# Four projection stages, a sampled convolution and a norm-and-gate stage rewritten: how their steps overlap, and how TensorE's array is divided

## The chip, the core and the metric

One NeuronCore of a Trainium2 chip runs the whole kernel as one launch. Its engines are TensorE (PE in the profile, with weight loads as PEld), VectorE (DVE), ScalarE (ACT), GpSimd (POOL) and SyncE (SP), which here only issues DMA. The metric is device time in microseconds (us), median of three runs. All data are float32. A float32 matmul stands in the profile as two PE records, so that "x2" of a 384-column matmul is one matmul of the program.

## The reference

Four residual layers run one after the other on x of shape 2 x 96 x 96 x 96 (two images, 96 channels, 9216 places). Each normalises by groups of three channels, goes through a selective scan in four directions and adds its output to x. What the change touches is this (cut to what matters):

```python
x = x + _L0_conv_ref(_gn(x), ...)      # layer 0: xz = in_proj(x); xs, z = split; 3x3 convolution,
                                       # batch norm, gelu, 1x1 to 2 offsets, grid_sample_bilinear, scans
x = x + _L1_conv_ref(_gn(x), ...)      # layer 1: layer norm, softmax gate, four mamba scans
x = x + _L2_conv_ref(_gn(x), ...)      # layers 2 and 3: in_proj, depthwise 3x3, four scans
x = x + _L3_conv_ref(_gn(x), ...)

def _gn(v, G=32, eps=1e-5):            # group statistics over 3 channels x 9216 places
    g = v.reshape(B_, G, C_ // G, H_, W_)
    return ((g - m) / jnp.sqrt(s + eps)).reshape(v.shape)

# layer 1, on the normalised tokens: layer norm over the 96 channels with gain and bias, then
# gate = softmax(w2 @ tanh(w1 @ x + b1) + b2) over 4 directions, w1: 24 x 96, w2: 4 x 24
```

## The kernel before

The stages of a layer run strictly one after another, each a `Phase` that ends with a barrier of all engines: statistics and projection, convolution, preparation of the scan's inputs, scan, merge, finish. Layer 1 has `norm_gate` ahead of its projection and no convolution stage of its own. SP issues all DMA, in program order, on one queue. The scans take most of the time and are the same in both kernels.

**Steps.** All stages here walk the 9216 places in 24 steps of N = 384 places (four image rows). The hidden width is 192 channels for each of two images; they lie in three tiles of 128 partitions: tile 0 is image 0's first 128 channels, tile 1 image 1's, and tile 2 holds the last 64 channels of image 0 in partitions 0 to 63 and of image 1 in 64 to 127. So a product that goes into or comes out of tile 2 uses half of the rows or half of the columns of PE's array, with zeros in the weights for the other half.

**`group_norm_head`** (L282, called by `norm_gate` and by three of the four projections) loads x (2 images, each in 2 halves) and takes `bn_stats` of 36 pieces of 512 places on DVE. All wait for all loads, on one semaphore.

**`project`** (L356, once a layer): each step scales x of both images on ACT (L419; in layer 1 it only copies, L417), then runs eight matmuls on PE (L437 to L440), four into `p_xs` and four into `p_z`, of which two each are tile 2's from image 0 and image 1. DVE copies `p_xs` to SBUF (L451), ACT takes silu of `p_z` (L425), both as one instruction over three banks, and SP stores both. ACT takes step s's silu before it scales step s + 1, and `p_xs` and `p_z` exist once.

**`conv_sampled`** (L556, layer 0): each step runs 63 matmuls of 384 columns (nine taps by seven blocks of `FEEDS`) into `p_conv` (L639), three gelus on ACT (L674), three matmuls into `p_off` (L647), tanh (L680), an affine step on POOL (L624), six matmuls that spread the offsets over partitions (`p_frac`, L657), and eight DVE instructions for each of three tiles (L709 to L727) that interpolate. PE goes through these in this order, and begins the next step's convolution after the spreads. The whole grid and the taps are loaded ahead of the first matmul.

**`norm_gate`** (L127, layer 1): for each step and each image, one after the other, with one buffer of each kind: scale (ACT), mean matmul (PE), subtract (DVE), square (ACT), variance matmul (PE), square root (ACT), reciprocal and product (DVE), gain and bias (ACT), hidden matmul (PE), tanh (ACT), three logit matmuls (PE), softmax (DVE, exp on ACT, DVE), three transposes (PE), copy (DVE). Each waits for the one ahead of it.

Of the kernel before, what the change touches and what calls it, by code (L numbers as in the profile page):

```python
# [10 lines left out]
ALU = mybir.AluOpType  # L11
ACT = mybir.ActivationFunctionType

P = 128
IMAGES = 2
# [12 lines left out]
GATE_HID = CH // 4  # L28
TAPS = 9
# [97 lines left out]
def norm_gate(nc, x_d, w, out_d, gate_d):  # L127

    with Phase(nc, "ng") as ph:
        x, scale, bias, loaded, stats = group_norm_head(nc, ph, x_d, w)  # L130
        N = SUB
        STEPS = L // N
        mean96 = ph.sb("mean96", [CH, CH])
        w1 = ph.sb("w1", [CH, GATE_HID])
        w2 = ph.sb("w2", [GATE_HID, DIRS])
        vecs = ph.sb("vecs", [CH, 2])
        b1 = ph.sb("b1", [GATE_HID, 1])
        b2 = ph.sb("b2", [P, DIRS])
        eye = ph.sb("eye", [P, P])
        xn = ph.sb("xn", [CH, N])  # L140
        xc = ph.sb("xc", [CH, N])
        sq = ph.sb("sq", [CH, N])
        sd = ph.sb("sd", [CH, N])
        rs = ph.sb("rs", [CH, N])
        xl = ph.sb("xl", [CH, 2, N])
        th = ph.sb("th", [GATE_HID, N])
        lg = ph.sb("lg", [P, 3, DIRS])
        mx = ph.sb("mx", [P, 3])
        sm = ph.sb("sm", [P, 3])
        gt = ph.sb("gt", [DIRS, 2, N])  # L150
        p_mean = ph.ps("p_mean", [CH, 512])
        p_var = ph.ps("p_var", [CH, 512])
        p_hid = ph.ps("p_hid", [GATE_HID, 512])
        p_log = ph.ps("p_log", [P, 3, DIRS])
        p_gt = ph.ps("p_gt", [DIRS, 512])
        weights = ph.sem("weights")
        eps_ready = ph.sem("eps_ready")
        act = ph.sem("act")
        dve = ph.sem("dve")
        pe = ph.sem("pe")  # L160
        xl_stored = [ph.sem(f"xl_stored{b}") for b in range(IMAGES)]
        gt_stored = [ph.sem(f"gt_stored{b}") for b in range(IMAGES)]
        A, D, E = 6, 13, 5
        eps = ph.sb("eps", [CH, 1])

        block_cm = ph.block()
        block = block_cm.__enter__()

        @block.sync
        def _(sp):  # L170
            for dst, src in ((mean96, w["mean96"]), (w1, w["gate_w1"]), (w2, w["gate_w2"]), (vecs, w["norm_gb"]),
                             (b1, w["gate_b1"]), (b2, w["gate_b2"]), (eye, w["eye"])):
                sp.dma_start(dst[:], src).then_inc(weights, 16)
            with sp.Fori(0, STEPS) as i:
                for b in range(IMAGES):

                    sp.wait_ge(act, i * (2 * A) + (b * A + 4) + ONE)
# [2195 lines left out]
```

## Time and profile before

| | us |
|---|---|
| median of 3 runs | 30857.21 (30854.06 to 30863.32) |
| the profiled execution | 30855.04 |
| its span | 30853.3 |
| PE busy in the span | 23829.2 |
| DVE busy in the span | 25538.5 |

The profiled execution's time is 1.7 us above its span and 2.2 us below the median. Since the stages are separated by barriers, the page's shares of the whole span say little about the stages changed here; each has to be read in its own stretch: layer 0's projection from 64 to 341 us, the sampled convolution from 392 to 1796, `norm_gate` from 8401 to 9304, layer 1's projection from 9308 to 9608. In a stretch, the columns give each engine's busy time, the granted PE clock as a share of full speed, and the busy share of the DMA engines.

### The profile page before, as it was taken

Reading aid. Unit: us, or ns where it says so; the run is one execution under the profiler, and the core shown is the slowest. Engines: PE = TensorE matmul, PEld = TensorE weight load, DVE = VectorE, ACT = ScalarE, POOL = GpSimd, SP = SyncE. Lnnn points to the kernel's source line nnn. Section 1 sums busy time; section 2 is a strip of 40 time slices with the busy share of each in tenths; the row PEclk is TensorE's granted clock in tenths of the full one; section 3 lists DMA queues with packets and bytes.
Section 4 is the critical chain, followed back from the end, with each engine's and each line's share of the span. In section 5 each row is a group of like instructions: output and inputs, shape, how many; then the busy total and the mean of one; then the engine's idle time right before and its main releaser. Section 6 shows DMA issues by size and latency. Waiting matters only on the chain. (4 is left out here: it accounts for less than half of the span.)

```text
span 30853.3 us, 332186 instructions
## 1 busy us (share of the span) xinstructions
PE 23829.2 (77%) x97030; PEld 7351.8 (24%) x97030; DVE 25538.5 (83%) x16489; ACT 14890.1 (48%) x20203; POOL 22839.6 (74%) x10221
## 2 busy tenths in 40 slices
PE   6877888888435688888886778888883778888885
PEld 3442222222112222222222422222221422222222
DVE  1259999999535999999993799999994689999995
ACT  1045555555134655555531555555551455555552
POOL 0028999999003699999992299999990189999991
PEclk8888888888756688888876888888886888888887
DMA  2042222221504422222235522222215532222224
GB/s 75 10 164 70 45 45 45 49 50 38 178 9 157 160 52 45 45 45 47 52 110 180 208 61 45 45 50 49 45 38 199 189 86 45 51 48 45 45 45 170
DMA packets 1155007, 2419.20 MB, mean 78 GB/s; under 512 B 118600, under 2 KB 656166, under 8 KB 1143680
## 3 DMA queue, kind: packets, MB, share of 16 engines
q1 hardware_dynamic: 1153224, 2397.86, 28.2%
q8 instruction: 821, 13.45, 0.2%
q14 instruction: 962, 7.88, 0.1%
HBM read 1374.43 MB, written 1023.05 MB: 78 GB/s over the span
## 5 line engine op out<-in xcount | busy, mean ns | idle before, releaser
L1355 POOL TENSOR_TENSOR scan_hc<-scan_bc,scan_h 128x1024 f32<-128x1024 f32 x6912 | 16086.7, 2362 | 108.3 <-DVE scan_h L1519 107.3
L1519 DVE TENSOR_TENSOR_SCAN scan_h<-scan_da,scan_state,scan_dbu 128x1024 f32<-128x1024 f32 x6912 | 15987.4, 2338 | 140.1 <-ACT scan_da L1407 133.9
L1438 PE MATMUL scan_da<-scan_dd,scan_ssel 32*128 32x512 f32 x27648 | 9101.0, 745 | 3013.1 <-DVE scan_h L1519 2781.0
L1407 ACT ACTIVATE scan_da<-scan_da,scan_a_cur 128x1024 f32<-128x1024 f32 x6912 | 7516.7, 1087 | 7720.6 <-PE scan_da L1438 7714.2
L1438 PE MATMUL scan_p_du<-scan_dd,scan_ssel 32*128 32x512 f32 x27648 | 9198.0, 745 | 534.2 <-DMA scan_bc<-bc_d 214.2
L1506 DVE TENSOR_TENSOR scan_dbu<-scan_p_du,scan_bc 128x1024 f32<-128x1024 f32 x4608 | 5561.0, 1207 | 506.1 <-PE scan_p_du L1438 475.5
L1341 POOL TENSOR_TENSOR scan_dbu<-scan_bc,scan_dus 128x1024 f32<-128x1024 f32 x2304 | 5446.0, 2364 | 145.7 <-ACT scan_dus L1381 145.1
L1438 PEld LDWEIGHTS scan_da<-scan_dd,scan_ssel 32*128 32x128 f32 x27648 | 2450.3, 216 | 10296.4 <-DVE scan_h L1519 8730.6
L1455 PE MATMUL scan_p_y<-scan_hc,scan_rsel 128*32 128x512 f32 x27648 | 4778.1, 772 | 17.2 <-POOL scan_hc L1355 16.8
L1438 PEld LDWEIGHTS scan_p_du<-scan_dd,scan_ssel 32*128 32x128 f32 x27648 | 2409.9, 211 | 3617.2 <-DVE scan_dbu L1506 2962.3
L1386 ACT ACTIVATE scan_state<-scan_h,scan_a_cur 128x1 f32<-128x1 f32 x6912 | 2025.1, 293 | 1584.3 <-DVE scan_h L1519 1476.4
L1381 ACT ACTIVATE scan_dus<-scan_p_du 128x1024 f32<-128x1024 f32 x2304 | 2358.5, 1024 | 217.2 <-PE scan_p_du L1438 170.1
L404 POOL MEMSET proj_xs_o<- 128x2352 f32 x4 | 8.2, 2058 | 2493.8 <-POOLq L69 2493.8
L835 POOL COPY prep_useq<-prep_grid 128x576 f32<-128x576 f32 (+1 forms) x480 | 581.3, 1263 | 1487.9 <-DMA du_d<-prep_useq 914.2
L1455 PEld LDWEIGHTS scan_p_y<-scan_hc,scan_rsel 128*32 128x32 f32 x27648 | 597.5, 119 | 3228.0 <-issue 2359.3
L639 PE MATMUL conv_p_conv<-conv_grid,conv_taps 128*128 x3024 | 1030.7, 504 | 52.6 <-DMA conv_grid<-xs_d 52.6
L624 POOL TENSOR_SCALAR conv_frac<-conv_frac 4x384 f32<-4x384 f32 x24 | 12.1, 504 | 1414.8 <-ACT conv_frac L680 1414.8
L451 DVE COPY proj_xs_o<-proj_p_xs 128x1152 f32<-128x1152 f32 x96 | 130.4, 1358 | 1006.8 <-PE proj_p_xs L440 1006.8
L845 PE MATMUL prep_p_dbl<-prep_useq,prep_wx 128*128 128x384 f32 x1728 | 805.1, 631 | 168.6 <-POOL prep_useq L835 168.6
L714 DVE TENSOR_TENSOR conv_top<-conv_diff,conv_p_frac 128x384 f32<-128x384 f32 x72 | 39.9, 554 | 1064.4 <-PE conv_p_frac L657 1062.7
L639 PEld LDWEIGHTS conv_p_conv<-conv_grid,conv_taps 128*128 128x128 f32 x3024 | 593.7, 197 | 500.2 <-issue 121.3
L1162 DVE SCALAR_TENSOR_TENSOR prep_useq<-prep_raw,prep_tapv,prep_useq 128x768 f32<-128x768 f32 x432 | 650.2, 1515 | 55.5 <-ACT prep_useq L1119 45.4
(215 smaller groups left out, 14787.6 us busy)
## 6 DMA issues: line engine op xcount, KB each, us to landing
scan_bc<-bc_d SPq DMA_DIRECT2D x576, 512.0 KB, 12.1
du_d<-prep_useq SPq DMA_DIRECT2D x384, 576.0 KB, 3.8
delta_d<-prep_delta SPq DMA_DIRECT2D x384, 576.0 KB, 4.3
scan_dd<-delta_d SPq DMA_DIRECT2D x1152, 192.0 KB, 4.9
scan_dd<-du_d SPq DMA_DIRECT2D x1152, 192.0 KB, 6.7
y_d<-scan_y SPq DMA_DIRECT2D x576, 384.0 KB, 5.8
merge_y<-y_d SPq DMA_DIRECT2D x384, 576.0 KB, 5.8
xs_d<-proj_xs_o SPq DMA_DIRECT2D x96, 588.0 KB, 3.3
```

Of the source, the lines that this page charges most:

```text
L639: last = nc.tensor.matmul(p_conv[:, m, 0:N], taps[:, tap, blk, :], grid[:, src, bass.ds(i * (2 * ROWS) + (j * ROWS + dy), ROWS), dx:dx + S ...
L845: last = nc.tensor.matmul(p_dbl[v % 2][:, 0:N], wx[:, v // (CHUNKS * PIECES), m, :], piece(v)[:, m, :], start=(m == 0), stop=(m == 2))
L1162: nc.vector.scalar_tensor_tensor(out=own, in0=raw[:, m, tap:tap + DW], scalar=tapv[:, m, tap:tap + 1], in1=own, op0=ALU.mult, op1=ALU.add) ...
L1341: nc.gpsimd.tensor_tensor(dbu[:, u % DBU_SLOTS, :], bc[:, s, image(u % UNITS), :], dus[:, u // TRIO % DUS_SLOTS, :], ALU.mult).then_inc(sh ...
L1355: nc.gpsimd.tensor_tensor(hc[:, u % HC_SLOTS, :], c, h[:, u % H_SLOTS, :], ALU.mult).then_inc(hc_ready, 1)
L1381: nc.scalar.activation(dus[:, u // TRIO % DUS_SLOTS, :], p_du[:], ACT.Copy).then_inc(share_copied, 1)
L1386: nc.scalar.activation(state[:, v % UNITS:v % UNITS + 1], h[:, v % H_SLOTS, T - 1:T], ACT.Copy, scale=a_cur[:, s, UNITS:UNITS + 1]).then_i ...
L1407: nc.scalar.activation(da[u % DELTA_BANKS][:], da[u % DELTA_BANKS][:], ACT.Exp, scale=a_cur[:, slot(u)[0], u % UNITS:u % UNITS + 1]).then_ ...
L1438: return nc.tensor.matmul(dst[:, half * H:(half + 1) * H], ssel[rows, i, :], dd[rows, s, m, j, :], start=True, stop=True)
L1455: last = nc.tensor.matmul(p_y[n % 2][at:at + QUAD, :], rsel[:, i, :], hc[:, v % HC_SLOTS, half * H:(half + 1) * H], start=(v % EIGHT < PAI ...
L1506: nc.vector.tensor_tensor(dbu[:, u % DBU_SLOTS, :], p_du[:], bc[:, slot(u)[0], image(u % UNITS), :], ALU.mult).then_inc(dbu_ready, 1)
L1519: nc.vector.tensor_tensor_scan(h[:, v % H_SLOTS, :], da[v % DELTA_BANKS][:], dbu[:, v % DBU_SLOTS, :], state[:, v % UNITS:v % UNITS + 1], ...
```

## The change

**Projection.** The eight PSUM banks are used in turn, one for each tile of a step (`bank_of`), each with its own semaphore count, so that PE runs on as soon as the bank of eight tiles ago is empty. Tile 2's two matmuls now write 64 columns each, in the two halves of the array's columns. ACT scales step s + 1 before step s's silus. In layer 1, x is not copied but read directly, and comes in four quarters, each with its semaphore. The stores have four buffers. All steps are written out.

**Sampled convolution.** `convolve_low` does tiles 0 and 1: for each tap two full matmuls and two of 64 rows each (tile 2 as the source), in the two halves of the array's rows. `convolve_high` does tile 2: for each tap two matmuls of 64 columns each and one full one. The offsets of step s - 1 come between low and high of step s, the spreads after high or between the two; the two spreads of a tile stand in rows 0 to 3 and 32 to 35. The grid is loaded in four bands, the first ahead of the taps.

**Norm and gate.** Scale and centring go into one matrix (`scaled_c`), the gain into the matrix that spreads the reciprocal (`gamma`), both images go together through most instructions, the reciprocal is taken of 2 rows in place of 96, and seven steps are in flight: turn t does the first part for step t and the last for step t - 6. There is a preamble that computes `scaled_c` and `shift`.

**Group statistics.** Each half of x has its own semaphore, so `bn_stats` begins with the first half.

In the part on `norm_gate` the three loops are those of TensorE, ScalarE and VectorE, in this order.

```diff
 def project(nc, l, x_d, w, xs_d, z_d, normed):
+        def bank_of(s, half, m):
+            return bank[(s * 2 * TILES + half * TILES + m) % BANKS]
...
-                            nc.tensor.matmul(psum[:, 0, 0:N], win[:, half, 0, :], xn[:, j, 0, :], start=True, stop=True)
-                            nc.tensor.matmul(psum[:, 1, 0:N], win[:, half, 0, :], xn[:, j, 1, :], start=True, stop=True)
-                            nc.tensor.matmul(psum[:, 2, 0:N], win[:, half, 1, :], xn[:, j, 0, :], start=True, stop=False)
-                            nc.tensor.matmul(psum[:, 2, 0:N], win[:, half, 2, :], xn[:, j, 1, :], start=False,
-                                             stop=True).then_inc(done, 1)
+                        for b in range(IMAGES):
+                            free(s, half, b)
+                            nc.tensor.matmul(bank_of(s, half, b)[:, 0:N], win[:, half, 0, :], src[b], start=True, stop=True).then_inc(done, 1)
+                        free(s, half, 2)
+                        for b in range(IMAGES):
+                            rows = slice(b * HALF, (b + 1) * HALF)
+                            last = nc.tensor.matmul(bank_of(s, half, 2)[rows, 0:N], win[:, half, 1 + b, rows], src[b], start=True, stop=True)
+                        last.then_inc(done, 1)
...
 def conv_sampled(nc, w, xs_d, u_d):
-        FEEDS = [[(0, 0), (2, 1)], [(1, 0), (2, 2)], [(0, 3), (1, 4), (2, 5)]]
...
+                def convolve_low(s):
+                    t.wait_ge(rows_loaded[band(s)], 16 + ONE)
+                    t.wait_ge(gelu_done, max(s * TILES - 1, 0) + ONE)
+                    for tap in range(TAPS):
+                        first, end = tap == 0, tap == TAPS - 1
+                        for m in range(2):
+                            nc.tensor.matmul(p_conv[:, m, 0:N], taps[:, tap, 0, :], rows_of(s, m, tap), start=first, stop=False)
+                        for m in range(2):
+                            half = slice(m * HALF, (m + 1) * HALF)
+                            last = nc.tensor.matmul(p_conv[:, m, 0:N], taps[half, tap, 1 + m, :], rows_of(s, 2, tap)[half],
+                                                    start=False, stop=end)
+                            if end:
+                                last.then_inc(conv_done, 1)
+                def convolve_high(s):
+                    t.wait_ge(gelu_done, s * TILES + ONE)
+                    for tap in range(TAPS):
+                        for m in range(2):
+                            half = slice(m * HALF, (m + 1) * HALF)
+                            nc.tensor.matmul(p_conv[half, 2, 0:N], taps[:, tap, 3 + m, half], rows_of(s, m, tap),
+                                             start=(tap == 0), stop=False)
+                        last = nc.tensor.matmul(p_conv[:, 2, 0:N], taps[:, tap, 5, :], rows_of(s, 2, tap), start=False,
+                                                stop=(tap == TAPS - 1))
+                    last.then_inc(conv_done, 1)
...
+                for s in range(STEPS + 2):
+                    if s < STEPS:
+                        convolve_low(s)
+                    if 0 <= s - 1 < STEPS:
+                        offsets(s - 1)
+                    if 0 <= s - 2:
+                        spread_offsets(s - 2, 2)
+                    if s < STEPS:
+                        convolve_high(s)
+                    if 0 <= s - 1 < STEPS:
+                        for m in range(2):
+                            spread_offsets(s - 1, m)
...
 def norm_gate(nc, x_d, w, out_d, gate_d):
+                for t in range(TURNS):
+                    if step(t):
+                        centre_x(t)
+                    if step(t - 1):
+                        square_sum(t - 1)
+                    if step(t - 2):
+                        spread(t - 2)
+                    if step(t - 3):
+                        hide(t - 3)
+                    if step(t - 4):
+                        make_logits(t - 4)
+                    if step(t - 6):
+                        transpose(t - 6)
...
+                for t in range(TURNS):
+                    if step(t - 1):
+                        deviation(t - 1)
+                    if step(t):
+                        square(t)
+                    if step(t - 2):
+                        add_beta(t - 2)
+                    if step(t - 3):
+                        hyperbolic(t - 3)
+                    if step(t - 4):
+                        exponential(t - 4)
...
+                for t in range(TURNS):
+                    if step(t - 5):
+                        soft_divide(t - 5)
+                    if step(t - 2):
+                        scale_x(t - 2)
+                    if step(t - 4):
+                        soft_shift(t - 4)
+                    if step(t - 1):
+                        invert(t - 1)
+                    if step(t - 6):
+                        take_gates(t - 6)
...
 def group_norm_head(nc, ph, x_d, w):
-                        d.wait_ge(loaded, 16 * 5 + ONE)
+                        d.wait_ge(half_loaded[2 * b + n // (NBN // 2)], 16 + ONE)
                         nc.vector.bn_stats(bn[:, b, n, :], x[:, b, n * BN:(n + 1) * BN]).then_inc(stats, 1)
```

On PE, the sampled convolution of a step stands as follows before (the numbers are output partitions x columns; `p_off` is 4 partitions high):

```order
L639 MATMUL conv_p_conv<-conv_grid,conv_taps 128x384 x29
L645 REGISTER_ALU
L647 MATMUL conv_p_off<-conv_gel,conv_off_w 4x384 x3
L650 ISA
L655 ISA
L657 MATMUL conv_p_frac<-conv_frac,conv_off_sel 128x384 x4
L655 REGISTER_ALU
L657 MATMUL conv_p_frac<-conv_frac,conv_off_sel 128x384 x2
```

Of the change, the same engine from the last taps of `convolve_low` of a step to the first of `convolve_high`, and the place where one step's high ends and the next step's low begins:

```order
L787 MATMUL conv_p_conv<-conv_grid,conv_taps 128x384 x2
L790 MATMUL conv_p_conv<-conv_grid,conv_taps 128x384 x2
L812 MATMUL conv_p_off<-conv_gel,conv_off_w 36x384 x3
L822 MATMUL conv_p_frac<-conv_frac,conv_off_sel 128x384 x2
L801 MATMUL conv_p_conv<-conv_grid,conv_taps 64x384 x2
L803 MATMUL conv_p_conv<-conv_grid,conv_taps 128x384
...
L803 MATMUL conv_p_conv<-conv_grid,conv_taps 128x384
L822 MATMUL conv_p_frac<-conv_frac,conv_off_sel 128x384 x4
L787 MATMUL conv_p_conv<-conv_grid,conv_taps 128x384 x2
```

The offsets and spreads have moved from the end of a step, where nothing else stood on PE, to places between the halves of the next one; and whole-array matmuls (L787, L803) now alternate with pairs in halves (L790, L801).

On ACT, one image of a step of `norm_gate` before, and one whole turn (both images) of the change:

```order
L196 ACTIVATE ng_xn<-ng_x,ng_gbias,ng_scale 96x384
L199 REGISTER_ALU
L200 ACTIVATE ng_sq<-ng_xc 96x384
L202 ISA
L203 ACT_TABLE_LOAD
L203 ACTIVATE ng_sd<-ng_p_var,ng_eps 96x384
L205 REGISTER_ALU
L206 ISA
L207 ACTIVATE ng_xl<-ng_xc,ng_vecs 96x384
L209 REGISTER_ALU
L210 ACT_TABLE_LOAD
L210 ACTIVATE ng_th<-ng_p_hid,ng_b 24x384
```

```order
L297 ACT_TABLE_LOAD
L297 ACTIVATE ng_sd<-ng_p_v,ng_eps 2x384
L305 ACTIVATE ng_xc<-ng_p_c,ng_shift 96x384
L306 ACTIVATE ng_sq<-ng_p_c,ng_shift 96x384
L305 ACTIVATE ng_xc<-ng_p_c,ng_shift 96x384
L306 ACTIVATE ng_sq<-ng_p_c,ng_shift 96x384
L313 ACTIVATE ng_xl<-ng_xr,ng_vecs 96x768
L319 ACT_TABLE_LOAD
L319 ACTIVATE ng_th<-ng_p_hid,ng_b 64x384
L323 ACTIVATE ng_lg<-ng_lg 128x24
```

The two table loads, which stood in each image's chain, now stand once a turn for both images, and the instructions of a turn belong to five different steps.

## Rows read from the trace of the kernel before

**Rows 1.** By stretch: us; PE, PEld, DVE, ACT, POOL busy (count); PE clock, DMA share, GB/s.

```profile
64.00:341.00 277.00, 186.19 (x384) 97.70 (x384) 32.58 (x24) 85.23 (x94) 0.00 (x0) 0.80 0.28 101
348.00:392.00 44.00, 0.00 (x0) 0.00 (x0) 0.00 (x0) 1.13 (x1) 0.60 (x2) 0.50 0.97 410
392.00:1796.00 1404.00, 1249.08 (x3456) 673.07 (x3456) 309.18 (x581) 70.33 (x109) 12.09 (x24) 0.90 0.03 10
8466.00:9304.00 838.00, 331.34 (x720) 120.40 (x720) 269.32 (x624) 311.90 (x408) 0.00 (x0) 0.50 0.03 9
9308.00:9345.00 37.00, 0.00 (x0) 0.00 (x0) 0.00 (x0) 0.59 (x1) 2.06 (x1) 0.50 0.92 199
9345.00:9608.00 263.00, 180.17 (x384) 94.37 (x384) 32.59 (x24) 77.53 (x96) 0.00 (x0) 0.80 0.28 105
16995.00:17186.00 191.00, 187.05 (x569) 105.57 (x567) 186.72 (x354) 37.43 (x69) 0.00 (x0) 1.00 0.29 112
```

**Rows 2.** Timeline of one projection step: start, duration, instruction, [idle before, releaser].

```profile
328.90 1.13 ACT L425 ACTIVATE proj_z_o<-proj_p_z 128x1152 f32<-128x1152 f32 x1
329.93 1.29 ACT L419 ACTIVATE proj_xn<-proj_x,proj_gbias,proj_scale 96x384 f32 x2
331.35 1.64 PE L437 MATMUL proj_p_xs<-proj_xn,proj_win 96*128 96x384 f32 x2 [3.85 <-ACT proj_xn L419]
340.15 1.13 ACT L425 ACTIVATE proj_z_o<-proj_p_z 128x1152 f32<-128x1152 f32 x1 [8.93 <-PE proj_p_z L440]
```

**Rows 3.** Timeline of the sampled convolution, PE, its first and last step.

```profile
392.67 42.62 PE L639 MATMUL conv_p_conv<-conv_grid,conv_taps 128*128 x126 [52.56 <-DMA conv_grid<-xs_d]
...
1727.85 42.34 PE L639 MATMUL conv_p_conv<-conv_grid,conv_taps 128*128 x126
1772.08 2.10 PE L647 MATMUL conv_p_off<-conv_gel,conv_off_w 128*4 128x384 f32 x6 [1.89 <-ACT conv_gel L674]
1775.59 2.84 PE L657 MATMUL conv_p_frac<-conv_frac,conv_off_sel 4*128 4x384 f32 x8 [1.42 <-POOL conv_frac L624]
```

**Rows 4.** Timeline, PE, layer 0's finish: rows*columns of the array.

```profile
8058.94 0.81 PE L1990 MATMUL fin_p_c<-fin_ym,fin_centre 128*128 128x384 f32 x2
8059.59 0.81 PE L1991 MATMUL fin_p_c<-fin_ym,fin_centre 128*128 128x384 f32 x2
...
8062.17 0.81 PE L1995 MATMUL fin_p_c<-fin_ym,fin_centre 128*128 128x384 f32 x2
8062.90 2.20 PE L2002 MATMUL fin_p_r<-fin_rs,fin_gamma 2*128 2x384 f32 x6
8065.03 0.89 PE L2010 MATMUL fin_p_o<-fin_t,fin_wo 128*96 128x384 f32 x2
```

**Rows 5.** Timeline, PE: groups in quarters of the array's rows and columns.

```profile
1908.47 2.84 PE L855 MATMUL prep_p_dt<-prep_dtv,prep_wdt 13*128 13x384 f32 x12 [1.73 <-ACT prep_dtv L876]
...
5007.87 1.07 PE L1455 MATMUL scan_p_y<-scan_hc,scan_rsel 128*32 128x512 f32 x8
```

**Rows 6.** Timeline, ACT: the nearest to the changed kernel's instructions.

```profile
436.68 1.80 ACT L674 ACTIVATE conv_gel<-conv_p_conv,conv_shift,conv_scale 128x384 f32<-128x384 f32 x3
...
1907.86 1.03 ACT L876 ACTIVATE prep_dtv<-prep_p_dbl,prep_ones 128x384 f32<-128x384 f32 x2
...
9700.66 1.01 ACT L1119 ACTIVATE prep_useq<-prep_raw,prep_conv_b,prep_tapv 128x768 f32<-128x768 f32 x1
```

**Rows 7.** Norm and gate: two steps' starts (timeline), then groups by line.

```profile
8466.99 0.71 ACT L196 ACTIVATE ng_xn<-ng_x,ng_gbias,ng_scale 96x384 f32 x1
...
8501.92 0.71 ACT L196 ACTIVATE ng_xn<-ng_x,ng_gbias,ng_scale 96x384 f32 x1
...
L203 ACT ACT_TABLE_LOAD x48 | 61.6, 1283 | 0.9
...
L255 DVE RECIPROCAL ng_rs<-ng_sd 96x384 f32<-96x384 f32 x48 | 122.3, 2549 | 136.9 <-ACT ng_sd L203 136.9
```

**Rows 8.** Timeline, DVE, head of the first projection.

```profile
35.11 21.45 DVE L315 BATCH_NORM_STATS2 proj_bn<-proj_x 96x6 f32<-96x512 f32 x36 [33.77 <-DMA proj_x<-in_x]
```

More of the change, by code:

```diff
@@ L294, in group_norm_head @@
     eps5 = ph.sb("eps5", [CH, 1])
-    loaded = ph.sem("x_loaded")
+    loaded = ph.sem("avg_loaded")
+    half_loaded = [ph.sem(f"x_loaded{n}") for n in range(2 * IMAGES)]
     stats = ph.sem("x_stats")
@@ new lines, in _ @@
+                if not normed:
+                    normalise(0)
+                for s in range(STEPS):
+                    if not normed and s + 1 < STEPS:
+                        normalise(s + 1)
+                    a.wait_ge(z_stored[s % DEEP], 16 * (s // DEEP) + ONE)
+                    for m in range(TILES):
+                        a.wait_ge(z_psum, s * TILES + m + 1 + ONE)
+                        nc.scalar.activation(z_o[:, s % DEEP, m, :], bank_of(s, 1, m)[:, 0:N], ACT.Silu).then_inc(z_ready, 1)
@@ new lines, in offsets, with spread_offsets @@
+                def offsets(s):
+                    t.wait_ge(gelu_done, (s + 1) * TILES + ONE)
+                    t.wait_ge(tanh_done, s + ONE)
+                    for m in range(TILES):
+                        last = nc.tensor.matmul(p_off[:, 0:N], off_w[:, m, :], gel[:, m, :], start=(m == 0), stop=(m == 2))
+                    last.then_inc(off_done, 1)
+                def spread_offsets(s, m):
+                    v = s * TILES + m
+                    t.wait_ge(frac_ready, s + 1 + ONE)
+                    t.wait_ge(lerp, max(v - 1, 0) * STEP + ONE)
+                    for axis in range(2):
+                        q = OFF_ROWS[axis]
+                        last = nc.tensor.matmul(p_frac[v % 2][:, axis, 0:N], off_sel[q:q + 2 * IMAGES, axis, m, :],
+                                                frac[q:q + 2 * IMAGES, s % 2, :], start=True, stop=True)
+                    last.then_inc(spread, 1)
@@ L661, in _, with gelu @@
             @block.scalar
             def _(a):
-                a.wait_ge(loaded, 16 * 7 + ONE)
+                def gelu(s, m):
+                    a.wait_ge(conv_done, s * TILES + m + 1 + ONE)
+                    a.wait_ge(off_done, s + ONE)
+                    nc.scalar.activation(gel[:, m, :], p_conv[:, m, 0:N], ACT.Gelu, bias=shift[:, m:m + 1],
+                                         scale=scale[:, m:m + 1]).then_inc(gelu_done, 1)
+                a.wait_ge(loaded, 16 * 4 + ONE)
                 a.wait_ge(consts, 1 + ONE)
```

612 lines of the change are left out of this document (342 added, 270 removed).

## The prediction

> **What bounds the kernel now.** I read first the busy times by stretch, then the timeline of a single step in each stretch, because barriers separate the stages: what a stage loses is lost outright, and what it gains is gained outright. The scans, preparations, merges and finishes are not touched, so I leave them at their times.
>
> In none of the changed stages does an engine work through. Layer 0's projection has PE busy 186 of 277 us at a mean granted clock of 0.80, ACT 85 and DVE 33, and the DMA engines 28% [rows 1]. The timeline says why: the silu of a step begins only 8.93 us after ACT's last work, when PE has finished; then ACT scales the next step, and PE waits 3.85 us for that [rows 2]. PE and ACT take turns, 24 times: 277 / 24 = 11.5 us a step.
>
> The sampled convolution has PE busy 1249 of 1404 us [rows 1]. Its 24 convolutions run from 392.67 to 1770.2 (1727.85 + 42.34), so 1377.5 us, with 23 tails between them [rows 3]. A step's 63 matmuls take 42.3 us; the period is (1770.2 - 435.3) / 23 = 58.0 us. The other 15.7 us are gelu, offsets, tanh, POOL's step, spreads and the interpolation that frees their banks, all in line.
>
> `norm_gate` is a pure chain: in 838 us PE is busy 331, ACT 312, DVE 269, and the clock is 0.50, the lower of its two levels (1.2 GHz), throughout [rows 1]. A step of both images takes 8501.92 - 8466.99 = 34.9 us [rows 7].
>
> **PE's prices, which carry the sum.** One matmul of 384 columns at full clock (2.4 GHz) takes 8059.59 - 8058.94 = 0.645 us when the next has the same shape. When the shape changes from 128*128 to 2*128, the step is 8062.90 - 8062.17 = 0.73, so 0.09 more; and the three matmuls of the new shape then take 2.13 us to the next group in place of 1.935, which is 0.20 more: 0.09 for leaving and 0.11 because the first weights of a new shape are loaded in the open [rows 4]. I take 0.20 us a change, and 0.15 where the new shape has 64 columns or fewer, since fewer weight columns are loaded; bounds are 0.09 and 0.20 for these. Whether a half of the array (64 rows or columns) counts as a new shape, no row shows; the bounds are 0 and 0.20, and I take 0.20, since the rows that change to a quarter are the nearest.
>
> Do halves run together? Twelve records of 13 rows each, six matmuls, take 2.84 us, where one after another they would take 3.87; the order in the code (rows 64, 96, 64, and again) allows four slots, 2.58. And eight records of 32 columns, four matmuls of 512 columns, take 1.07 us, where the same in turn would take four times 0.86 [rows 5]. I take full overlap: a pair costs one slot of 0.645.
>
> Here the Trainium skill has a rule that speaks against the change: TensorEngine Tiling (Array Packing), section Tiling Modes, says that changing the tiling mode, not just the tile, drains TensorE. The trace agrees, with the 0.20 us above. By the page's table of speedups alone (up to 2 times for 64 rows or columns, nothing for changes) the time would be that of the first rival.
>
> **Sampled convolution.** Per tap, low has 2 full matmuls and a pair, high a pair and a full one: 5 slots in place of 7, so 45 a step; offsets 3, spreads 3 (a pair each): 51 slots, 32.9 us. Changes of shape: 18 in low, 18 in high, 1 for the offsets, 2 for spreads: 39, of them 10 at 0.15, so 7.3 us. That is 40.2 us a turn, in place of 58.0. Does anything stop PE? Low of step s needs gelu of tiles 0 and 1 of s - 1, done during high; high needs tile 2's gelu of s - 1, done during low; the spreads come some 15 us after the offsets, and the chain between them was 3.5 us (1775.59 - 1772.08) [rows 3]. DVE's 309 us in all [rows 1] are 12.9 a step. So PE runs through, and stays at full clock: a stretch of 191 us that runs through had 1.00 [rows 1]. 24 x 40.2 = 965, less 3 for the first turn, which has no offsets, plus 2 for its first matmuls at half clock: 964 against 1377.5, **413 saved**. The tail after the last convolution stays. The start: all 17.9 MB were awaited, 44 us at 410 GB/s [rows 1]; now one band of four and the taps, 7.2 MB, 18 us and a landing: **24 saved**.
>
> **Projections of layers 0, 2 and 3.** Six slots, 3.87 us, and four changes (two at 0.15), 0.70: 4.57 a step. Beside it ACT has two scalings (1.29, [rows 2]) and three silus (three gelus of the same size take 1.80, [rows 6]), 3.1 us, and DVE three copies (33 us / 24 = 1.36 as one, some 1.6 as three). The stores: 28% of 277 / 24 is 3.2 us of DMA time a step. All are under 4.57, so PE is the bound. A bank is wanted again after eight tiles, 6 us later. 24 x 4.57 = 110, 3.5 for the first 7 us at half clock, 1 for the last silu: 114 against 277. 3 x 163 = **489 saved**. POOL's zeroing is twice as long (four pieces), some 2 us more, and lies beside the first scalings.
>
> **Layer 1's projection.** PE did nothing in the stage's first 37 us, while both images landed at 199 GB/s, and then the steps took 263 [rows 1]. A quarter of x lands after 9 us and the weights ahead of it after 2: PE starts 26 us earlier. The steps take 114, as above: 149 saved. The first stores queue behind the last quarters of x, until some 36 us in; step 4 wants the first store's buffer at about that time, so I charge 4. 149 + 26 - 4 = **171 saved**.
>
> **Norm and gate.** ACT's turn: two table loads 2.57, square root and tanh 0.57 each at most (0.60 by the gelus), four of centre and square at 0.515 (1.03 for two), gain and bias over 768 columns 1.01, exp 0.2: 7.0 us [rows 6, 7]. PE's turn at full clock: seven slots (the pair for both images counts once) 4.5, six small matmuls 1.1, six changes 0.8: 6.4 us. DVE: the reciprocal of 2 rows is as long as that of 96, 2.55 [rows 7], now once for both images, and some 2.8 more: 5.4. The binding loop is ACT alone; the loop through PE (last square, centring, sum of squares, root, squares again) is 0.2 + 1.3 + 0.2 + 1.3 + 0.6 + 2.1 = 5.7. So 7.0 a turn; PE at 6.4 of 7.0 stays nearly always busy, and I take full clock after the first turns. 24 x 7.0 = 168, 14 for six draining turns (a chain of one step), 6 for the start at half clock: 188; preamble and three more loads 3. 838 - 191 = **647 saved**.
>
> A page says otherwise on the table loads: ScalarE: Activation LUTs, What ACT_TABLE_LOAD costs, gives 1283 ns and a drain of 1380 for each switch. The trace has the 1283 but only 0.9 us of idle ahead of all 48 [rows 7], so it doesn't agree on the drain; by the page the stage would be 66 us longer.
>
> **Heads.** x lands over 33.8 us, then 36 pieces take 21.45 [rows 8]. Now three quarters of that lie beside the load, and 5.4 are left: 16 us, four times, **64 saved**.
>
> Sum: 413 + 24 + 489 + 171 + 647 + 64 = 1808. From the profiled execution's 30855.0 that is 29047; the median was 2.2 higher, so 29049. I predict 29050.
>
> **The rivals.**
> *Halves are no new shape* (12%). For it: all rows that show a change go to a quarter or less of the rows or columns. Against: nothing in particular but that the drain is there at all. Then the 17 changes inside low and the 17 inside high cost nothing, 6.4 us a turn, 154, and 0.70 x 96 = 67 in the projections: 28830.
> *Halves don't overlap* (8%). Against it are both rows of 5; for it, that they show quarters. It costs 18 slots a convolution turn, 279, and 2 a projection step, 124: 29450.
> *PE stays at 1.2 GHz in `norm_gate`* (12%). For it: the clock was 0.50 for 838 us [rows 1], and small matmuls and changes are gaps of a kind. Then PE's turn is 12.8 us and binds: 24 x 5.8 = 139 more, 29190.
> *Slower than before* (2%): a change of shape between half and whole arrays costs far more than one to a quarter. There are 39 x 24 + 4 x 96 = 1320 of them; to eat 1808 us each must cost 1.4 us more than the 0.2 taken. From 1.6 us on it decides. At 1.8 us the kernel would take 31150. Rows 4 show nothing near it.
>
> My forecast has 66%, with its own range 28930 to 29180 (ACT's or PE's turns 5% off). **Range** at 8 in 10: 28790 to 29310; it takes in the clock rival, and the first at its edge, and leaves out the second and the last. What a measurement of this kernel can tell from no change is about 0.2%, 62 us: faster 0.97, same 0.01, slower 0.02.
>
> **What would show it.** In the profile after: convolution turns of 40 us with PE running through at clock 1.00, and steps of 0.73 to 0.85 us where L790 follows L787; projection steps of 4.6 us; `norm_gate` turns of 7 us with ACT busy throughout. I'd be wrong if L787 follows L790 at 0.645, if a pair takes 1.29, or if in a projection PE waits for banks (L575 behind L550).

## The result, and the profile after

The changed kernel takes 29517.14 us (median of 4 runs, 29504.46 to 29548.98) against 30855.64 of the kernel before (4 runs, 30836.15 to 30863.32): ratio 0.9568, 95% interval 0.9553 to 0.9584. That is 1338 us less where 1808 were forecast. The time lies 207 us above the forecast range.

The profiled execution took 29522.75 us (span 29520.9), 1332 less than that of before. The stages are separated by barriers, so each difference can be read by itself, from a stage's first to its last instruction:

| stage | before, us | after, us | saved | forecast |
|---|---|---|---|---|
| four heads | 59.1, 59.4, 59.2, 59.0 | 42.6, 42.1, 42.5, 43.0 | 66 | 64 |
| sampled convolution | 1446.5 | 1011.4 | 435 | 437 |
| projections 0, 2, 3 | 283.8, 282.9, 284.2 | 215.2 each | 205 | 489 |
| projection 1 | 304.7 | 223.7 | 81 | 171 |
| `norm_gate` behind its head | 844.8 | 254.7 | 590 | 647 |
| all the others | | | -45 | 0 |

Two lines are right to 2 us. The projections miss 374 us between them, `norm_gate` 57, and the stages that nobody touched are 45 us longer; together that is the gap.

The windows of the changed kernel answer to [rows 1]. The columns are the same: PE, PEld, DVE, ACT and POOL busy with counts, granted clock, DMA share, GB/s.

```profile
291.10:1245.00 953.90, 953.90 (x3420) 352.29 (x3420) 289.74 (x528) 54.79 (x95) 11.68 (x23) 1.00 0.06 23
7955.00:8202.00 247.00, 236.63 (x602) 84.65 (x602) 116.91 (x220) 152.44 (x235) 0.00 (x0) 0.60 0.10 30
8218.00:8427.00 209.00, 208.14 (x384) 70.71 (x384) 40.16 (x72) 36.03 (x72) 0.00 (x0) 0.50 0.47 159
15486.00:15694.00 208.00, 207.85 (x384) 70.71 (x384) 40.16 (x72) 62.20 (x116) 1.50 (x2) 0.50 0.36 135
```

PE now works through in the convolution and the projections, as intended: 953.90 of 953.90 us in the one, 208.14 of 209.00 and 207.85 of 208.00 in the others; in `norm_gate` it is busy 236.63 of 247.00. But the clock column differs. The convolution has 1.00; the projections have 0.50 from end to end, the lower level (1.2 GHz). Before, with PE idle for a third of the same stage and every matmul of the one shape 96*128, the projections had a mean of 0.80 [rows 1]. `norm_gate` has 0.60.

The timeline of PE in layer 2's projection is the answer to [rows 2]. A step is now two groups of full columns and two pairs of halves. (A *slot* below is the time of one matmul of 384 columns, a *change* a change of shape, that is of the rows*columns in use.)

```profile
15549.72 1.55 PE L579 MATMUL proj_bank<-proj_xn,proj_win 96*64 96x384 f32 x4
15551.20 2.93 PE L575 MATMUL proj_bank<-proj_xn,proj_win 96*128 96x384 f32 x4
15554.06 1.55 PE L579 MATMUL proj_bank<-proj_xn,proj_win 96*64 96x384 f32 x4
15555.53 2.93 PE L575 MATMUL proj_bank<-proj_xn,proj_win 96*128 96x384 f32 x4
15558.39 1.55 PE L579 MATMUL proj_bank<-proj_xn,proj_win 96*64 96x384 f32 x4
```

No row shows an idle time, so PE waits for no bank and no operand. Start to start, a step takes 15558.39 - 15549.72 = 8.67 us, where 4.57 were forecast. (A record is half a matmul here: x4 are two matmuls of full columns, or one pair.) The pair begins at 15549.72 and the full ones at 15551.20, 1.48 later: it takes one slot, not two, at a slot of 1.28 us at this clock, and 0.20 for the change. Halves do lie side by side. (Over the whole step the four changes take 8.67 - 6 x 1.28 = 0.99 us at this clock, some 0.25 each.)

The convolution, against [rows 3]: a part of low, and the spreads that end a turn.

```profile
604.16 1.56 PE L787 MATMUL conv_p_conv<-conv_grid,conv_taps 128*128 128x384 f32 x4
605.65 0.92 PE L790 MATMUL conv_p_conv<-conv_grid,conv_taps 64*128 64x384 f32 x4
606.49 1.56 PE L787 MATMUL conv_p_conv<-conv_grid,conv_taps 128*128 128x384 f32 x4
607.98 0.92 PE L790 MATMUL conv_p_conv<-conv_grid,conv_taps 64*128 64x384 f32 x4
...
642.81 1.56 PE L822 MATMUL conv_p_frac<-conv_frac,conv_off_sel 4*128 4x384 f32 x8
```

Two full matmuls and the change to a pair take 605.65 - 604.16 = 1.49 us, which is 2 x 0.645 + 0.20; the pair and the change back take 0.84, which is 0.645 + 0.20. These are the prices of the forecast. The next turn begins at 642.81 + 1.49 = 644.30, so a turn is 40.14 us; 40.2 was forecast.

### The profile page after: what moved, and what is told of

It reads as the page before. It is cut to its first block and busy times, and to the rows that moved or that the text cites. A ratio compares the mean times of both kernels' runs of the same rounds, so it can differ in the third digit from the quotient of the medians.

```text
span 29520.9 us, 327473 instructions
## 1 busy us (share of the span) xinstructions
PE 23564.0 (80%) x96912; PEld 6910.2 (23%) x96912; DVE 25423.2 (86%) x16276; ACT 14602.1 (49%) x20071; POOL 22855.8 (77%) x10233
## 5 line engine op out<-in xcount | busy, mean ns | idle before, releaser
L590 DVE COPY proj_xs_o<-proj_bank 128x384 f32<-128x384 f32 x288 | 160.6, 558 | 688.7 <-PE proj_bank L575 599.4
L1035 PE MATMUL prep_p_dt<-prep_dtv,prep_wdt 13*128 13x384 f32 x1728 | 499.8, 590 | 256.9 <-ACT prep_dtv L1056 256.1
L1767 DVE TENSOR_TENSOR merge_acc<-merge_acc,merge_y 128x576 f32<-128x576 f32 (+1 forms) x480 | 532.0, 1144 | 157.2 <-DMA merge_y<-y_d 66.9
L1083 DVE TENSOR_TENSOR prep_delta<-prep_p_dt,prep_softplus 128x1152 f32<-128x1152 f32 x288 | 377.6, 1353 | 326.3 <-ACT prep_softplus L1067 326.3
```

## The experiments

All are edits of the changed kernel. Only e9, e10 and e11 leave work out. "Projection time" below is PE's, from its first to its last instruction in the stage: 208.2 us in each projection of the changed kernel.

The question was why the clock stays low in a stage in which PE never pauses. Two families of reasons were on the table: the halves and their changes of shape (A), or the 96 rows of 128 (B). The first four runs take one of these away each.

**e1: tile 2 by matmuls of all columns.**

```
-   for b in range(IMAGES):
-       rows = slice(b * HALF, (b + 1) * HALF)
-       last = nc.tensor.matmul(bank_of(s, half, 2)[rows, 0:N], win[:, half, 1 + b, rows], src[b], start=True, stop=True)
+   for b in range(IMAGES):
+       last = nc.tensor.matmul(bank_of(s, half, 2)[:, 0:N], win[:, half, 1 + b, :], src[b], start=(b == 0), stop=(b == 1))
```

> The changed kernel (29517 us) with tile 2 of all four projections made by two accumulating matmuls of all 128 columns in place of two halves side by side: 8 slots a step, one shape, no change of shape. Theory A (the half columns and their changes of shape hold TensorE at 1.2 GHz): the granted clock in the projections rises to 1.00 and a step takes 8 x 0.645 = 5.2 us in place of 8.67; 24 x 3.5 x 4 = 336 less, about 29180. Theory B (a TensorE that runs through on 96 rows stays at 1.2 GHz, whatever the columns): clock 0.50, a step is 8 x 1.28 = 10.3 us, 24 x 1.6 x 4 = 154 more, about 29670.

**e2: the full matmuls of a step first, then both pairs.**

```
    for half, done in ((0, xs_psum), (1, z_psum)):
        for b in range(IMAGES):
            free(s, half, b)
            nc.tensor.matmul(bank_of(s, half, b)[:, 0:N], win[:, half, 0, :], src[b], start=True, stop=True).then_inc(done, 1)
+   for half, done in ((0, xs_psum), (1, z_psum)):
        free(s, half, 2)
...
```

> The changed kernel with the four matmuls of all columns of a projection step first and then its two pairs of halves: the same matmuls, 2 changes of shape a step in place of 4. Theory A1 (the changes hold the clock down): with half of them gone the clock rises, to 1.00 in the best case, a step is 3.87 + 0.35 = 4.2 us, up to 430 less, about 29090. Theory A2 (the halves themselves do, by their share of the work) and theory B (96 rows): clock 0.50, and the step loses only two changes, 8.67 to some 8.3 us, 35 less, about 29480.

**e3: every matmul in halves of the columns.**

```
-   nc.tensor.matmul(bank_of(s, half, b)[:, 0:N], win[:, half, 0, :], src[b], start=True, stop=True).then_inc(done, 1)
+   for c in range(2):
+       cols = slice(c * HALF, (c + 1) * HALF)
+       last = nc.tensor.matmul(bank_of(s, half, b)[cols, 0:N], win[:, half, 0, cols], src[b], start=True, stop=True)
+   last.then_inc(done, 1)
```

> The changed kernel with every matmul of the projections in halves of the columns, always side by side: six slots a step, twelve matmuls, no change of shape at all. Theory A1 (changes): clock 1.00, a step is 6 x 0.645 = 3.9 us; 24 x 4.8 x 4 = 460 less, about 29060. Theory A2 (halves) and theory B (96 rows): clock 0.50, a step is 6 x 1.28 = 7.7 us; 24 x 1 x 4 = 93 less, about 29425. If halves of equal shape should not lie side by side at all, 15 us a step and about 30100.

**e4: 128 rows, of which 32 are zeros.**

```
-   xn = ph.sb("xn", [CH, 2, IMAGES, N])
+   xn = ph.sb("xn", [P, 2, IMAGES, N])      # x in layer 1, and win, likewise
+   nc.vector.memset(xn[CH:P], 0.0).then_inc(padded, 1)
```

> The changed kernel with the projections' operands padded from 96 to 128 rows by zeros (x or its scaled copy, and the weights); shapes, halves and changes stay in number and place. Theory B (96 rows of 128 hold the clock down): clock 1.00 in the projections, as in the convolution that has the same mixture on 128 rows, a step of 4.6 us, 24 x 4.1 x 4 = 390 less, about 29125. Theory A (halves or changes): clock 0.50, a step of 8.67 us, about 29520 (plus a few us for the zeros). If only active rows with data that toggles count, zeros change nothing either, and this run then does not exclude B.

Measured, beside the changed kernel's 29517.14 us (ratios are to the kernel before, with 95% intervals):

| run | us | ratio | changes a step | projection time, layers 0 to 3 |
|---|---|---|---|---|
| changed kernel | 29517.14 | 0.9568 (0.9553, 0.9584) | 4 | 208.2, 208.2, 208.2, 208.2 |
| e1 | 29205.34 | 0.9465 (0.9449, 0.9481) | 0 | 126.4, 127.3, 126.3, 126.3 |
| e2 | 29114.04 | 0.9433 (0.9417, 0.9449) | 2 | 107.6, 107.4, 115.6, 103.3 |
| e3 | 29076.81 | 0.9422 (0.9406, 0.9438) | 0 | 96.4, 100.4, 95.5, 94.9 |
| e4 | 29147.68 | 0.9445 (0.9430, 0.9461) | 4 | 111.8, 111.9, 111.7, 112.2 |

Neither family won: e1 to e3 came out as theory A said, e4 as theory B said, so each cure works alone. The windows of one projection in each run, in the order e1, e3, e4, show the clock back near 1.00 with the stage still run through:

```profile
15330.37:15456.63 126.26, 126.25 (x384) 73.97 (x384) 40.16 (x72) 62.07 (x116) 1.27 (x2) 0.98 0.59 220
```

```profile
15270.08:15365.54 95.46, 95.46 (x576) 41.03 (x576) 40.16 (x72) 62.08 (x116) 1.30 (x2) 0.97 0.78 289
```

```profile
15320.14:15431.86 111.72, 111.72 (x384) 42.59 (x384) 40.16 (x72) 62.04 (x116) 0.89 (x1) 0.98 0.66 248
```

e4 is the cleanest, because it has the same matmuls in the same order as the changed kernel. Its timeline in layer 2:

```profile
15349.59 1.56 PE L577 MATMUL proj_bank<-proj_xn,proj_win 128*128 128x384 f32 x4
15351.08 0.87 PE L581 MATMUL proj_bank<-proj_xn,proj_win 128*64 128x384 f32 x4
15351.87 1.56 PE L577 MATMUL proj_bank<-proj_xn,proj_win 128*128 128x384 f32 x4
15353.36 0.87 PE L581 MATMUL proj_bank<-proj_xn,proj_win 128*64 128x384 f32 x4
15354.16 1.56 PE L577 MATMUL proj_bank<-proj_xn,proj_win 128*128 128x384 f32 x4
```

A step is 15354.16 - 15349.59 = 4.57 us, exactly the sum of the forecast (six slots and four changes). So the forecast's slots, overlap and change prices hold here too; only the clock that they were priced at was wrong. The other runs' steps fit the same prices: 5.16 us in e1 (8 x 0.645), 3.87 in e3 (6 x 0.645), 4.22 in e2 (3.87 and two changes).

e2 is the one that is not all at full clock. The windows of its layer 2 projection, split where the level changes:

```profile
15300.00:15329.00 29.00, 29.00 (x55) 12.25 (x56) 6.14 (x11) 9.48 (x17) 1.05 (x2) 0.50 0.34 124
15329.20:15415.00 85.80, 85.80 (x330) 38.93 (x328) 33.66 (x61) 52.56 (x99) 0.00 (x0) 1.00 0.75 276
```

With two changes a step the level rose 29 us after PE's first matmul in this stage, and 13, 12 and 4 us after it in layers 0, 1 and 3; in e1, e3 and e4 it rose after 4 to 7 us in every layer; with four changes on 96 rows it did not rise in 208 us. So the changes work by degrees, and two a step already show. Nor does e3 owe its clock to halves being gone: it has nothing but halves. The halves themselves are acquitted.

The next three runs test the reading that was left: rows and changes of shape add up.

**e9: 64 rows and no change of shape.** It leaves out a third of the 96 channels. Layers 0 and 2 in halves as e3, layers 1 and 3 in full columns as e1.

```
-   src = [xn[:, s % 2, b, :] for b in range(IMAGES)]
+   src = [xn[0:ROWS_IN, s % 2, b, :] for b in range(IMAGES)]      # ROWS_IN = 64; x in layer 1, and win, likewise
```

> Leaves work out: the projections use only 64 of the 96 rows (channels) of x and of the weights. In layers 0 and 2 every matmul of the projection is in halves of the columns (no change of shape), in layers 1 and 3 every one is of all columns (no change, 8 slots a step). The stages run through as before. Theory S (the granted level follows how much of the array works on the mean: rows, times columns, less the gaps of the changes): 64 rows without any gap work less than 96 rows with four changes did, so the clock is 0.50: steps of 6 x 1.28 = 7.7 us in layers 0 and 2 (184 us of projection) and 8 x 1.28 = 10.2 in layers 1 and 3 (246 us). Theory C (only changes of shape hold the clock down, rows don't matter by themselves, and the 128 rows helped by chance or by the margin): clock 1.00, 3.9 and 5.2 us a step, some 95 and 126 us of projection, as with 96 rows.

Measured: 29543.73 us (one run). The windows of the projections of layers 1 and 2:

```profile
8192.63:8438.73 246.10, 246.09 (x384) 127.68 (x384) 40.17 (x72) 36.03 (x72) 0.00 (x0) 0.50 0.40 134
15498.48:15683.07 184.59, 184.59 (x576) 67.40 (x576) 40.17 (x72) 62.24 (x116) 1.24 (x2) 0.50 0.41 152
```

Both forecasts of theory S (184 and 246 us at 0.50) are met to a microsecond, those of theory C missed by 90 and 120. A single run does for this, since what is read is the level and the step in one stage. Fewer rows hold the clock down by themselves: PE is never idle here and never changes shape.

**e10: the convolution on 96 rows. e11: the same, with the taps regrouped as in e7 (below).** Both leave out 32 of the 128 rows in the matmuls of all rows.

```
-   nc.tensor.matmul(p_conv[:, m, 0:N], taps[:, tap, 0, :], rows_of(s, m, tap), start=first, stop=False)
+   nc.tensor.matmul(p_conv[:, m, 0:N], taps[0:CH, tap, 0, :], rows_of(s, m, tap)[0:CH], start=first, stop=False)      # CH = 96; high likewise
```

> Leaves work out: the changed kernel's sampled convolution uses only 96 of 128 rows in the matmuls of all rows (the pairs of half the rows keep their 64 and 64); order, halves and the 39 changes of shape a turn stay. Theory S (mean working share, rows and gaps together): what the projections showed repeats in another stage, in part at least: the convolution had 1.00 on 128 rows; on 96 with 0.75 changes a slot it falls to 0.50 or swings between the levels; at 0.50 throughout a turn is 51 x 1.28 + 39 x 0.25 = 75 us in place of 40.1, the convolutions 1800 us in place of 959, the kernel 30360. Rival (it was something of the projections: their stores, banks or operands): clock 1.00, a turn of 40.1 us, about 29520.

> Leaves work out in the same way: the convolution on 96 of 128 rows, but with the taps regrouped so that a turn has some 6 changes of shape in place of 39. Theory S: 96 rows with few gaps keep the full clock, as in the projections all in halves: a turn of 34 us as on 128 rows, about 29375. Theory B (96 rows by themselves): clock 0.50, 51 x 1.28 + 2 = 67 us a turn, about 30170.

Measured: 29545.02 and 29375.53 us (one run each). The windows of e10 over one dip and the stretch behind it, and of e11 over its convolutions:

```profile
486.00:489.40 3.40, 3.40 (x8) 1.06 (x6) 3.25 (x6) 0.00 (x0) 0.00 (x0) 0.50 0.00 0
489.40:567.90 78.50, 78.50 (x284) 29.01 (x283) 23.06 (x43) 4.55 (x8) 1.01 (x2) 1.00 0.04 16
```

```profile
292.60:1108.40 815.80, 814.49 (x3436) 417.23 (x3434) 294.31 (x537) 55.95 (x97) 12.45 (x24) 1.00 0.07 26
```

Direction right, size far off. In e10 the clock drops to 0.50 for 3.4 us ten times, every 81.9 us, while PE works through; on 128 rows with the same 39 changes it dropped not once (1.00 over the 953.90 us above), and on 96 rows with few changes not once either (e11). PE's time in the stage rises from 978.9 to 997.2 us, 18 us, where the expectation had up to 840. So rows and changes act together in this stage too, but far more weakly than in the projections, although it has more changes for its slots (39 in 51, against 4 in 6). One difference is known: a third of low (the pairs of 64 and 64 rows) kept all 128 rows. Whether that accounts for the size is open.

**e5: `norm_gate`'s means and deviations on 96 rows and columns.**

```
-   mean = ph.sb("mean", [CH, IMAGES, IMAGES])        gamma = ph.sb("gamma", [IMAGES, IMAGES, CH])
+   mean = ph.sb("mean", [CH, IMAGES, CH])            gamma = ph.sb("gamma", [CH, IMAGES, CH])
-   p_v = ph.ps("p_v", [IMAGES, 512])                 sd, rs, eps on IMAGES partitions
+   p_v = ph.ps("p_v", [CH, 512])                     sd, rs, eps on CH partitions
```

> The changed kernel (29517 us) with norm_gate's mean, standard deviation and its reciprocal on 96 rows (94 of them idle numbers), so that centring, sum of squares and spread are matmuls of one shape, 96*96: 4 changes of shape a turn in place of 6, and no matmul of 2 rows or 2 columns. ACT's and DVE's work is the same. Theory A (how much of the array works, on the mean, sets the level): the granted clock of 0.60 rises to near 1.00, a turn comes from some 9.3 to 7.0 us, ACT's own sum, 24 x 2.3 = 50 less, about 29465. Rival (the small matmuls of the gate hold the clock at 1.2 GHz by themselves): clock about 0.6, only the two changes are saved, 12 less, within the scatter.

Measured: 29444.82 us, ratio 0.9538 (0.9523, 0.9552). The windows of e5's `norm_gate` in its steady part and at its end, and PE's timeline of one turn:

```profile
7953.10:8099.90 146.80, 132.49 (x538) 63.55 (x536) 106.30 (x187) 142.42 (x218) 0.00 (x0) 1.00 0.17 47
8099.90:8117.00 17.10, 13.64 (x45) 6.55 (x45) 8.90 (x29) 3.80 (x9) 0.00 (x0) 0.50 0.14 39
```

```profile
8040.71 1.53 PE L227 MATMUL ng_p_c<-ng_x,ng_scaled_c 96*96 96x384 f32 x4 [0.52 <-ACT ng_sq L306]
8042.08 1.45 PE L235 MATMUL ng_p_v<-ng_sq,ng_mean 96*96 96x384 f32 x4
8043.37 1.45 PE L243 MATMUL ng_p_r<-ng_rs,ng_gamma 96*96 96x384 f32 x4
8044.75 0.84 PE L252 MATMUL ng_p_hid<-ng_xl,ng_w 96*32 96x384 f32 x4
...
8047.29 1.53 PE L227 MATMUL ng_p_c<-ng_x,ng_scaled_c 96*96 96x384 f32 x4 [0.52 <-ACT ng_sq L306]
```

The stage falls from 254.7 to 188.5 us (66 less; 50 were expected), within 3 us of the forecast's 191. (Left as it is, the stage took between 254.7 and 269.9 us in the profiled executions of the changed kernel and the other runs, so 66 is the least that the edit gives.) The edit alters two things at once, the rows and columns in use and two changes of shape, and doesn't tell them apart. A turn is 8047.29 - 8040.71 = 6.58 us, and ACT is busy 142.42 of 146.80 us: it is the bound that the forecast named. It is reached only with the clock at 1.00. In the changed kernel the level swings, as two windows show, and in the slow part PE, not ACT, is full:

```profile
8060.00:8070.00 10.00, 9.94 (x42) 3.85 (x41) 6.00 (x12) 8.79 (x15) 0.00 (x0) 1.00 0.11 32
8070.00:8097.00 27.00, 27.00 (x61) 9.71 (x61) 12.89 (x23) 17.14 (x28) 0.00 (x0) 0.50 0.12 35
```

**e6: the halves of the convolution undone. e7: its taps regrouped.**

```
    e6: taps[half, tap, 1 + m, :], rows_of(s, 2, tap)[half]  ->  taps[:, tap, 1 + m, :], rows_of(s, 2, tap)
        p_conv[half, 2, 0:N], taps[:, tap, 3 + m, half]      ->  p_conv[:, 2, 0:N], taps[:, tap, 3 + m, :]
    e7: for tap: full, full, pair          ->  for tap: full, full;  for tap: pair      (low)
        for tap: pair, full                ->  for tap: pair;        for tap: full      (high)
```

> The changed kernel with the halves of the sampled convolution undone: 63 matmuls of all rows and columns a step again, in the new order of stages. It prices halves and their changes together at full clock: 63 + 3 + 3 = 69 slots are 44.5 us and 5 changes 0.9, so 45.4 us a turn in place of 40.14: 24 x 5.2 = 125 more, about 29640. So of the 419 us that the convolution gained, 294 would be the overlap of stages and 125 the halves. Rival: the overlap alone does nearly all, since 34 changes eat the halves: a turn of 41 us, 20 more.

> The changed kernel with the convolution's taps regrouped: low has its 18 full matmuls and then its 9 pairs, high its 9 pairs and then its 9 full ones; the same matmuls, some 6 changes of shape a turn in place of 39. If each change costs 0.15 to 0.20 us wherever it stands: 33 x 0.185 = 6.1 us a turn, 24 x 6.1 = 146 less, a turn of 34.1 us, about 29370. If gelus or spreads now come too late (DVE has 12.9 us of work a turn, the chain offsets, tanh, POOL's step is 3.5): a turn of 36 or more. If most of the steps of 0.80 to 0.85 us are no changes but something that every pair has, nothing: 40 us.

Measured: e6 29640.16 us, ratio 0.9606 (0.9591, 0.9621); e7 29377.05, ratio 0.9516 (0.9502, 0.9531). Two turns' starts in e6, from PE's timeline:

```profile
600.86 1.56 PE L787 MATMUL conv_p_conv<-conv_grid,conv_taps 128*128 128x384 f32 x4
...
646.30 1.56 PE L787 MATMUL conv_p_conv<-conv_grid,conv_taps 128*128 128x384 f32 x4
```

e6's turn is 45.44 us (45.4 expected), the stage 1138.4 in place of 1011.4: of the 435 us, 127 are the halves, net of the changes that they bring, and 308 the overlap and the earlier start. In e7, PE's time in the stage falls from 978.9 to 835.8 us, 5.96 a turn (6.1 expected). Its timeline of one turn:

```profile
602.48 6.08 PE L791 MATMUL conv_p_conv<-conv_grid,conv_taps 64*128 64x384 f32 x36
608.49 2.13 PE L814 MATMUL conv_p_off<-conv_gel,conv_off_w 128*36 128x384 f32 x6
610.54 0.91 PE L824 MATMUL conv_p_frac<-conv_frac,conv_off_sel 4*128 4x384 f32 x4
611.39 6.03 PE L802 MATMUL conv_p_conv<-conv_grid,conv_taps 128*64 128x384 f32 x36
617.34 6.07 PE L805 MATMUL conv_p_conv<-conv_grid,conv_taps 128*128 128x384 f32 x18
623.35 1.56 PE L824 MATMUL conv_p_frac<-conv_frac,conv_off_sel 4*128 4x384 f32 x8
624.84 11.88 PE L786 MATMUL conv_p_conv<-conv_grid,conv_taps 128*128 128x384 f32 x36
636.65 5.75 PE L791 MATMUL conv_p_conv<-conv_grid,conv_taps 64*128 64x384 f32 x34
```

These are seven groups and so seven changes, one more than the expectation counted: 32 of the 39 are gone, at 5.96 / 32 = 0.19 us each on the mean.

**e8: e3, e5 and e7 together.**

> The version that joins what the runs point to: projections in halves of the columns throughout, norm_gate with wide mean and deviation, the convolution's taps regrouped. If the three are independent: 29077 - 146 - 50 = 28880, ratio 0.936 to the kernel before. If norm_gate keeps its clock at 0.6: 28930. If the regrouping gives nothing: 29030.

Measured: 28854.18 us (5 runs, 28845.18 to 28866.74), ratio 0.9348 (0.9335, 0.9361); 663 us, 2.2%, less than the changed kernel. The three add up: the stages of e8 take 868.6 (convolution), 188.8 (`norm_gate`) and 102, 116, 103, 102 us (projections), the same as in the runs of one edit. This is the best version of the study. Its convolution and layer 2's projection:

```profile
173.42:1009.49 836.07, 825.22 (x3456) 422.87 (x3456) 309.31 (x569) 56.14 (x98) 12.45 (x24) 0.99 0.08 29
...
15042.68:15138.15 95.47, 95.47 (x576) 41.14 (x576) 40.16 (x72) 62.03 (x116) 1.19 (x2) 0.97 0.78 289
```

## Why the prediction was wrong, step by step

- **The step that failed** is "24 x 4.57 = 110, 3.5 for the first 7 us at half clock" for the projections, taken over for layer 1's ("The steps take 114, as above"). PE is the bound; but 4.57 us supposes full clock, and the paragraph gives no reason for that. The nearest reason in the prediction stands under the convolution: "a stretch of 191 us that runs through had 1.00". That stretch was layer 2's depthwise convolution, whose matmuls in the trace of before are all 128*128, without a change of shape; it says that running through can be enough, not that it is. No rival was written for the clock in the projections. The step measured 8.67 us at 0.50, which is 24 x 4.1 = 98 us a projection, or 393 for four. The stages' shortfall is 374; of the difference, 14 are the 3.5 us at half clock, charged four times, which the 8.67 holds already. With 128 rows and nothing else changed (e4), the step was 4.57.
- **Norm and gate**: the mechanism (ACT binds, some 7.0 us a turn) was right wherever the clock was full (e5; that its stage came within 3 us is in part luck, since 24 turns at 6.58 are 158 us where 168 were charged, and what stands around them took 31 where 23 were); "I take full clock after the first turns" was not. The rival with half clock throughout was priced at 139 us more than the forecast; the level swung, at a mean of 0.60, and the cost was 57. The table loads kept the price of [rows 7], with little idle time around them: ACT, with two loads a turn, is busy 142.42 of 146.80 us in e5. The clock rival had been written for this one stage. The thought behind it, that small matmuls and changes weigh on the clock, belonged to the projections first, where nothing covered PE's time.
- **Sampled convolution**: right in nearly each term: turn 40.14 (40.2), convolutions 419 us shorter (413), first matmul 21.6 us after the stage's start in place of 45.0, 23 saved (24). "The tail after the last convolution stays" was off by 8 us, which happens to cancel the 6 gained above: DVE finished 27.6 us after the last convolution where it was 20 before, since PE's last spreads wait for DVE's interpolations of the step before:

```profile
1254.50 1.65 PE L822 MATMUL conv_p_frac<-conv_frac,conv_off_sel 4*128 4x384 f32 x4 [3.80 <-DVE conv_u_o L907]
```

- **Halves**: a half is a new shape (0.84 us where L787 follows L790, not 0.645) and halves do overlap (twelve matmuls in 3.87 us in e3); both rivals on that are out. The prices of 0.15 to 0.20 us a change were taken from changes to few rows [rows 4], and carried over at full clock.
- **Heads**: 66 us saved for 64.
- **The stages nobody touched** took 45 us more, 32.5 of them in the scans. Layer 3's scan is 22 of that, here after and then before:

```profile
23476.24:28891.87 5415.63, 4514.96 (x20736) 1125.96 (x20736) 5230.57 (x2880) 2994.11 (x4287) 5322.08 (x2305) 0.86 0.22 46
```

```profile
24830.69:30223.77 5393.08, 4513.77 (x20736) 1121.11 (x20736) 5229.70 (x2880) 2995.11 (x4287) 5321.67 (x2305) 0.86 0.22 47
```

DVE and POOL, which bind it, are busy for the same time to within 1 us; the 22 us are idle time. The scan has the same code in both, and in the profiled executions of e1 to e8 it took between 5414 and 5435 us. Scatter alone can be large: layer 1's scan, with the same code too, took 5407 us before, and between 5393 and 5433 in the changed kernel and those runs. But layer 3's was longer in every one of them than in the one profile of before. Why is open; no experiment was made on it.

One rule bears on the failed step. The Trainium skill, TensorE: Matmul & The Clock Gate, section Part 1: The HAM clock gate, says that the clock follows how busy PE has recently been and that sustained matmuls release it. The runs agree for one shape on 96 rows (e1: 0.98), and not for the changed kernel, whose PE was busy 208.14 of 209.00 us at 0.50, nor for e9, busy 184.59 of 184.59 at 0.50. Busy in the profile's sense was not enough in these stages; the measurement decides.

What stays open is how rows and changes are weighed against each other. The means of a stage don't order the runs: on 96 rows, the kernel before had 0.80 with PE idle for a third and no change, the changed kernel 0.50 with PE never idle and changes that take 0.99 of 8.67 us. The runs show their signs (fewer rows lower the level, changes of shape lower it, halves side by side do not) and that two moderate amounts together did what neither did alone; e10's size shows that these signs don't make a formula.

## What to carry to other kernels

Before a stage is priced at full clock, compare it with a stretch of the trace that has the same rows and the same changes of shape, and not only the same absence of gaps; price both levels where there is none, since the factor is nearly two for anything that PE binds (8.67 against 4.57 us a step). Where a stage runs on 96 rows, keep it to one shape: cut all matmuls in halves, or order them by shape (each change costs 0.15 to 0.20 us besides), or fill up the rows with zeros; here each of these gave back 93 to 113 us of PE's 208 in a projection (e3, e2, e4). On 64 rows one shape was not enough: e9 stayed at 0.50; zeros in the other rows were not tried there. And check the granted clock stage by stage after every change that makes PE busier: a page that shows PE busy 100% may show it busy at half speed.

## What the runs showed of the hardware that was not expected

- PE busy without a gap for 208 us at a granted clock of 0.50 (96 rows, four changes of shape in 8.67 us), while the kernel before, idle for a third of the same stage, had 0.80.
- Rows that hold only zeros raise the level too: e4's clock is 0.98, with the same data otherwise.
- 64 rows without any change of shape: 0.50 (e9); 96 rows without any: 0.97 and 0.98 in layer 2 (e3, e1).
- A matmul cut in two halves of the columns costs nothing: e3 has twelve matmuls in 3.87 us, six slots of 0.645.
- With the steps that short, PE no longer works through in layer 1's projection in e3. The DMA engines are at 0.97, PE waits once, 2.29 us, for a bank that DVE has to empty, and right behind that wait the level is 0.50 for 3.4 us. The window and the wait:

```profile
8110.81:8211.23 100.42, 98.13 (x576) 43.49 (x576) 39.66 (x72) 35.38 (x72) 0.00 (x0) 0.95 0.97 323
...
8137.07 1.06 PE L582 MATMUL proj_bank<-proj_x,proj_win 96*64 96x384 f32 x4 [2.29 <-DVE proj_xs_o L593]
```
